# A fused attention and mixture-of-experts kernel: the head of its first pass in another order

## The reference

```python
q = query @ Wq.T + bq;  k = key @ Wk.T + bk;  v = value @ Wv.T + bv
att = where(masks, q @ k.T / sqrt(d), -1e9)
x = x + tanh(g_xattn) * (softmax(att) @ v)      # query = layernorm(x), key = value = ctx
x = x + tanh(g_ffn) * (routed_experts(layernorm(x)) + shared_expert(layernorm(x)))
```

## Time and profile before

| | |
|---|---|
| median of 3 runs | 1158.11 us (1152.9 to 1160.1) |
| profiled execution | 1157.58 us, span 1155.8 us |
| PE busy | 1050.2 us (91%) |
| DVE busy | 822.7 us (71%) |
| ACT busy | 531.4 us (46%) |
| POOL busy | 441.8 us (38%) |
| granted TensorE clock, mean | 0.953 |

### The profile page before, as it was taken

One profiled execution on the slowest core, in us unless ns is written; L12 is line 12 of the kernel. 1 busy time (PEld: TensorE's weight loads), 2 busy tenths in 40 slices (PEclk: granted clock), 3 DMA queues, 4 the chain that ended last, 5 costly groups with the idle time before them and its releaser, 6 DMA issues.

```text
span 1155.8 us, 26617 instructions
## 1 busy us (share of the span) xinstructions
PE 1050.2 (91%) x7344; PEld 677.3 (59%) x7345; DVE 822.7 (71%) x2938; ACT 531.4 (46%) x1041; POOL 441.8 (38%) x654
## 2 busy tenths in 40 slices
PE   4699979999999999860899999999999999999997
PEld 3488767777777777660455555555554444444443
DVE  5899868788888888763576666666665666666666
ACT  1366546666666666640444444444443232232322
POOL 3254647676667667442112112112110423232322
PEclk9999889999999999855899999999999999999999
DMA  7555573223323223432233333333332544444543
GB/s 290 197 177 179 131 173 95 93 93 93 93 93 94 94 93 110 101 102 72 74 110 118 115 113 118 118 109 118 118 109 67 185 158 161 157 168 149 169 149 128
DMA packets 76731, 146.96 MB, mean 127 GB/s; under 512 B 20912, under 2 KB 23088, under 8 KB 73872
## 3 DMA queue, kind: packets, MB, share of 16 engines
q1 hardware_dynamic: 46512, 66.01, 20.0%
q10 hardware_dynamic: 17280, 44.83, 10.5%
q0 software_dynamic: 12896, 35.58, 9.9%
HBM read 94.04 MB, written 52.35 MB: 127 GB/s over the span
## 4 chain that ended last, share of the span: by engine, by line
PE 64%; issue 11%; DVE 9%; POOL 8%; ACT 4%; DMA 2%; POOLq 1%; another core or an unknown queue 1%; SPq 0%; DVEq 0%; ACTq 0%
PE bank L1046 15%; PE bank L1047 15%; PE bank L1048 15%; PE bank L1038 8%; PE bank L1090 3%; PE bank L1108 3%; DVE arena L776 3%; POOL arena L467 3%; POOL token_of_row L503 2%; ACT arena L605 1%; DVE arena L865 1%; POOL arena L474 1%; DMA token_of_row<-arena 1%; DVE peak L879 1%; PE bank L1064 1%
## 5 line engine op out<-in xcount | busy, mean ns | idle before, releaser
L1046 PE MATMUL bank<-weights,arena 128*128 (+1 forms) x682 | 259.9, 381 | 2.1 <-ACT arena L647 1.9
L1047 PE MATMUL bank<-weights,arena 128*128 (+1 forms) x682 | 259.8, 381 | 0.0
L1048 PE MATMUL bank<-weights,arena 128*128 (+1 forms) x682 | 259.6, 381 | 0.0
L1038 PE MATMUL bank<-ident,arena 128*128 128x128 f32 (+1 forms) x1592 | 189.4, 267 | 56.1 <-DMA arena<-normed_rows,arena 25.7
L1038 PEld LDWEIGHTS bank<-ident,arena 128*128 128x128 f32 (+1 forms) x1592 | 161.4, 132 | 103.0 <-issue 71.9
L514 POOL DMA_INDIRECT arena<-normed_rows,arena x71 | 67.1, 946 | 254.9 <-PE bank L1038 238.7
L1108 PEld LDWEIGHTS bank<-arena 128*128 128x128 f32 x1024 | 131.7, 198 | 34.3 <-issue 29.5
L1090 PE MATMUL bank<-arena 128*128 128x512 f32 x256 | 138.8, 647 | 5.4 <-DVE arena L776 5.1
L1108 PE MATMUL bank<-arena 128*128 128x33 f32 x1024 | 128.8, 276 | 2.9 <-issue 1.8
L467 POOL TENSOR_TENSOR arena<-arena 128x512 f32<-128x512 f32 x96 | 101.3, 1056 | 76.8 <-DVE arena L776 75.7
L524 POOL DMA_INDIRECT arena<-expert_rows,arena x64 | 62.8, 981 | 173.9 <-DVE arena L998 156.1
(11 more groups left out here) (175 smaller groups left out, 1895.7 us busy)
## 6 DMA issues: line engine op xcount, KB each, us to landing
expert_rows<-arena ACTq DMA_DIRECT2D x71, 256.0 KB, 2.1
arena<-in_x SPq DMA_DIRECT2D x64, 256.0 KB, 3.2
weights<-in_w_gu ACTq DMA_DIRECT2D x8, 1024.0 KB, 4.7
x_rows<-arena SPq DMA_DIRECT2D x32, 256.0 KB
normed_rows<-arena SPq DMA_DIRECT2D x32, 256.0 KB, 4.9
normed_transposed<-arena SPq DMA_DIRECT2D x32, 256.0 KB, 2.3
arena<-normed_transposed SPq DMA_DIRECT2D x32, 256.0 KB, 3.3
arena<-x_rows SPq DMA_DIRECT2D x32, 256.0 KB, 3.4
```

The source lines that it names most:

```text
L1038: last = t.transpose(dst[:, c * P:(c + 1) * P], src[:, c * P:(c + 1) * P], (ident16 if src.dtype == F16 else ident)[:, :])
L1046: t.matmul(dst, hi[:, rows], w_hi(c), start=(c == 0), stop=False)
L1047: t.matmul(dst, hi[:, rows], w_lo(c), start=False, stop=False)
L1048: last = t.matmul(dst, lo[:, rows], w_hi(c), start=False, stop=(c == chunks - 1))
```

## The change: what it does

SP loads the query weights first, then the small inputs, then context and key weights; the value weights are issued in SP's `beside(1)`, behind the first two tiles. PE computes the keys into banks 2 to 5, then goes straight into the pipeline, and computes the values into banks 6 and 7 in `beside(2)`, after the queries of tile 0. The waits for the low query weights, the router weights, the keys and the values stand at the first product that reads each. DVE makes the low parts of the router and query weights in `beside(0)`, after the statistics of tile 0, and evicts keys and values in `beside(2)`. The reading of the expert chunks starts at iteration 3 in place of 2, so it ends at iteration 11 in place of 10, and ACT's loads of them move by one iteration as well.

```diff
+        K_BANK = 2
-        PEAK_AT, peak_counts = 2, [2, 2, 2, 2, 2, 1, 1, 1, 1]
+        PEAK_AT, peak_counts = 3, [2, 2, 2, 2, 2, 1, 1, 1, 1]
 # SyncE
-            sp.dma_start(ctx_s, ctx_t).then_inc(kv_in, 16)
-            sp.dma_start(wk_s, wk_t).then_inc(kv_in, 16)
+            sp.dma_start(wq_raw, wq_t.rearrange("p c n -> p (c n)")).then_inc(wq_in, 16)
             for dst, src in ((gate_raw[:, :], gates), (bq_s[:, :], bq), (bk_s[:, :], bk), (bv_s, bv),
                              (router_s[:, :, :], router), (pad_raw[:, :, :], pad)):
                 sp.dma_start(dst, src).then_inc(small_in, 16)
-            sp.dma_start(wq_raw, wq_t.rearrange("p c n -> p (c n)")).then_inc(wq_in, 16)
-            sp.dma_start(wv_s, wv_t).then_inc(v_in, 16)
+            sp.dma_start(ctx_s, ctx_t).then_inc(kv_in, 16)
+            sp.dma_start(wk_s, wk_t).then_inc(kv_in, 16)
             def beside(it):
+                if it == 1:
+                    sp.dma_start(wv_s, wv_t).then_inc(v_in, 16)
 # VectorE
-            dve.wait_ge(router_hi, 1)
-            d.scalar_tensor_tensor(router_w[:, 1], ...).then_inc(router_lo, 1)
-            dve.wait_ge(prep_hi, 1)
-            d.scalar_tensor_tensor(wq[:, 1, :], ...).then_inc(prep_lo, 1)
+            def query_weights():
+                dve.wait_ge(router_hi, 1)
+                d.scalar_tensor_tensor(router_w[:, 1], ...).then_inc(router_lo, 1)
+                dve.wait_ge(prep_hi, 1)
+                d.scalar_tensor_tensor(wq[:, 1, :], ...).then_inc(prep_lo, 1)
             def keys_and_values():
-                        d.tensor_scalar(kbd[...], bank[c][...], ...)
+                        last = d.tensor_scalar(kbd[...], bank[K_BANK + c][...], ...)
+                last.then_inc(kv_set, 1)
                 dve.wait_ge(kv_mm, 2)
-                    last = d.tensor_tensor(vaug[:, b, :, 0:D], bank[4 + b][:, :]..., ALU.add)
+                    last = d.tensor_tensor(vaug[:, b, :, 0:D], bank[6 + b][:, :]..., ALU.add)
                 last.then_inc(kv_set, 1)
-                if it == 1:
+                if it == 0:
+                    query_weights()
+                if it == 2:
                     keys_and_values()
 # TensorE
-                    last = t.matmul(bank[co][:, 0:B * T], wk_s[...], ctx_s[:, ci, :], ...)
+                    last = t.matmul(bank[K_BANK + co][:, 0:B * T], wk_s[...], ctx_s[:, ci, :], ...)
             last.then_inc(kv_mm, 1)
-            pe.wait_ge(v_in, 16)
-            for b in range(B):
-                for ci in range(EC):
-                    last = t.matmul(bank[4 + b][:, :], ctx_s[...], wv_s[:, ci, :], ...)
-            last.then_inc(kv_mm, 1)
-            pe.wait_ge(const_set, 11)
-            pe.wait_ge(kv_set, 2)
-            pe.wait_ge(prep_lo, 1)
-            pe.wait_ge(router_lo, 1)
+            def values():
+                pe.wait_ge(v_in, 16)
+                for b in range(B):
+                    for ci in range(EC):
+                        last = t.matmul(bank[6 + b][:, :], ctx_s[...], wv_s[:, ci, :], ...)
+                last.then_inc(kv_mm, 1)
                 # scores(k)
+                        if it_is_first(n, k):
+                            pe.wait_ge(kv_set, 2)
                 # mix_values(k)
+                        if it_is_first(n, k):
+                            pe.wait_ge(kv_set, 3)
                 # queries(chunks)
+                        if it_is_first(n, chunks[0]):
+                            pe.wait_ge(prep_lo, 1)
                 # router
+                    if it_is_first(n6, 0):
+                        pe.wait_ge(router_lo, 1)
+            def it_is_first(n, k):
+                return isinstance(n, int) and n == 0 and k == 0
             def beside(it):
+                if it == 2:
+                    values()
```

More of the change, by code:

```diff
@@ L745, in _ @@
             scale_of(4, 6, 19)
-            dve.wait_ge(router_hi, 1)
-            d.scalar_tensor_tensor(router_w[:, 1], router_s[:, :, :], w_scale[:, 4:5], router_w[:, 0], ALU.mult, ALU.subtract).then_inc(router_lo, 1)
-            dve.wait_ge(prep_hi, 1)
-            d.scalar_tensor_tensor(wq[:, 1, :], wq_raw, w_scale[:, 0:1], wq[:, 0, :], ALU.mult, ALU.subtract).then_inc(prep_lo, 1)
+            def query_weights():
+                dve.wait_ge(router_hi, 1)
+                d.scalar_tensor_tensor(router_w[:, 1], router_s[:, :, :], w_scale[:, 4:5], router_w[:, 0], ALU.mult, ALU.subtract).then_inc(router_lo, 1)
+                dve.wait_ge(prep_hi, 1)
+                d.scalar_tensor_tensor(wq[:, 1, :], wq_raw, w_scale[:, 0:1], wq[:, 0, :], ALU.mult, ALU.subtract).then_inc(prep_lo, 1)
             def keys_and_values():
@@ L756, in keys_and_values @@
                         rows = slice(h * D, (h + 1) * D)
-                        d.tensor_scalar(kbd[rows, :, c, h * T:(h + 1) * T], bank[c][rows, 0:B * T].rearrange("p (b t) -> p b t", b=B),
-                                        bk_s[rows, c:c + 1], float(D) ** -0.5, ALU.add, ALU.mult)
+                        last = d.tensor_scalar(kbd[rows, :, c, h * T:(h + 1) * T], bank[K_BANK + c][rows, 0:B * T].rearrange("p (b t) -> p b t", b=B),
+                                               bk_s[rows, c:c + 1], float(D) ** -0.5, ALU.add, ALU.mult)
+                last.then_inc(kv_set, 1)
                 dve.wait_ge(kv_mm, 2)
                 for b in range(B):
-                    last = d.tensor_tensor(vaug[:, b, :, 0:D], bank[4 + b][:, :].rearrange("p (h d) -> p h d", h=H),
+                    last = d.tensor_tensor(vaug[:, b, :, 0:D], bank[6 + b][:, :].rearrange("p (h d) -> p h d", h=H),
                                            bv_s.rearrange("p (h d) -> p h d", h=H), ALU.add)
@@ L1063, in _ @@
                 for ci in range(EC):
-                    last = t.matmul(bank[co][:, 0:B * T], wk_s[:, ci, co * P:(co + 1) * P], ctx_s[:, ci, :],
+                    last = t.matmul(bank[K_BANK + co][:, 0:B * T], wk_s[:, ci, co * P:(co + 1) * P], ctx_s[:, ci, :],
                                     start=(ci == 0), stop=(ci == EC - 1))
             last.then_inc(kv_mm, 1)
-            pe.wait_ge(v_in, 16)
-            for b in range(B):
-                for ci in range(EC):
-                    last = t.matmul(bank[4 + b][:, :], ctx_s[:, ci, b * T:(b + 1) * T], wv_s[:, ci, :],
-                                    start=(ci == 0), stop=(ci == EC - 1))
-            last.then_inc(kv_mm, 1)
-            pe.wait_ge(const_set, 11)
-            pe.wait_ge(kv_set, 2)
-            pe.wait_ge(prep_lo, 1)
-            pe.wait_ge(router_lo, 1)
+            def values():
+                pe.wait_ge(v_in, 16)
+                for b in range(B):
+                    for ci in range(EC):
+                        last = t.matmul(bank[6 + b][:, :], ctx_s[:, ci, b * T:(b + 1) * T], wv_s[:, ci, :],
+                                        start=(ci == 0), stop=(ci == EC - 1))
+                last.then_inc(kv_mm, 1)
             def body(J, v):
```

## The result

The changed kernel takes 1151.88 us (median of 15 runs, 1148.6 to 1155.2) against 1158.29 of the kernel before in the same comparison (15 runs): ratio 0.9948, 95% interval 0.9927 to 0.9968, so between 3.7 and 8.5 us faster; the medians lie 6.4 apart. That is inside the 1% that was called no change, and close to the 7.3 that the forecast took off. The profiled execution took 1153.63 us with a span of 1151.9, 3.9 shorter than that of before.

A forecast was written before the change was run, and what follows sets the result against it. PE, busy 91% of the span, was taken as the bound, with gains in the head's chain of waits: -10.3 for the head, +1.4 for iteration 7 and +1.6 for the turn gave 1151 us, range 1144.5 to 1158.

The forecast's parts named there:

- part 1: Head, loads: with query weights first and the keys' operands last, keys start at 11.6 instead of 16.00, 4.4 us gained.
- part 2: Head, PE's moved waits: tile 0's rows and the low query weights arrive in time, with slack 3.7 and 5.5, costing nothing.
- part 3: Head: full-speed queries, then values, with evictions under PE's work; DVE starts tile 1 at 33.7, 10.3 us gained including the loads' 4.4.
- part 4: Chunks one iteration later: iteration 7 costs 1.4 us (bounds 0 and 2.27), the turn in iteration 11 costs 1.6 (0 to 3.1).
- The sum: Whole kernel: -10.3 + 1.4 + 1.6 = -7.3 us, giving 1150.3 on the profiled execution and 1150.8 on the median.
- the 1.6 put down for the turn: Turn of the scales, iteration 11: PE and ACT wait 1.6 us more behind the moved chunk, the middle of 0 to 3.1.
- the signs that the forecast named: Wrong if the lead at iteration 3 is under 8, the turn costs over 3, or the lead shrinks in the loop.
- (a): First tile: the clock stays low, costing 1.8 us in the queries and as much in the values, 1154.6; chance 0.15.
- (b): DVE or ACT streams: pauses at new places; one more gives 1155, two 1159.8, slower than before; chance 0.07.
- (c): More gain: one of two pauses disappears and iteration 11's chunk is hidden, 1145.7, or 1144.3 with iteration 7 free; chance 0.2.
- (d): Head: the overlap does not come, only the loads' gain is left, -1.4 us in all, 1156.7; chance 0.08.
- The rule that calls fetches mostly hidden: DVE's and ACT's pauses: by the skill neither is an instruction fetch, and iteration 11's extra chunk costs a plain 1.6 us.

The follow-up runs named there:

- e6: Changed kernel with ScalarE's first pair of chunk loads issued in iteration 2 instead of 1; ratio 0.9988 to the kernel before.
- e7: Changed kernel with the old order of SyncE's loads, so the new order of work alone; ratio 0.9979 to the kernel before.
- after_again: Changed kernel unaltered, run again on another chip; ratio 0.9985 to the kernel before, profiled execution 1156.30 us.
- e10: Changed kernel without the indirect writes of token numbers and the waits for them, so its data are wrong; ratio 0.9634 to the kernel before.
- e2: Kernel before with only the chunk reads and loads moved one iteration later; ratio 1.0041, 4.8 us slower.
- e4: Changed kernel with ScalarE's 3 MB of chunk reloads issued behind the turn of the scales, not in iteration 10; ratio 0.9918 to the kernel before.
- before_again: Kernel before, unaltered, a single run on the chip of the changed kernel's second measurement; profiled execution 1162.63 us.
- e9: Changed kernel with key evictions and chunk reads reordered into VectorE's gaps and the 3 MB reloads behind the turn; ratio 0.9879 to the kernel before.
- e5: Kernel before with only ScalarE's 3 MB of chunk reloads issued behind the turn of the scales; ratio 0.9943, 6.7 us faster on its chip.

## Why the prediction was right, step by step

**Loads (part 1)**: right. Keys start at 11.96 where 11.6 was forecast. The argument that the same bytes are ahead of the key weights as had been ahead of the query weights held to 0.4.

**Waits of PE (part 2)**: right. Tile 0's transposes start as the keys end; no moved wait showed.

**Queries, values and evictions (part 3)**: the mechanism was right, its size 1.7 too large. The step that failed is "from about 23.4, the 16 key evictions", started there as if tile 2's statistics had their rows. I wrote of ACT's moved loads "Nothing", and looked only at whether they come in time for DVE. What they do to the transfer beside them was the missing term: 7.3 us for 256 KB, against 2.5 for tile 4's rows, asked for at 39.46 with no large load just ahead. The profile of before had the row for it: there tile 2's rows, asked for at 24.86 behind ACT's loads of 24.02 and 24.39, landed after 7.1 us, hidden beside the evictions. e6 shows the term by taking it away (1.8 against e4), e7 by having it with other loads.

**Chunks later (part 4)**: right for iteration 8, too low by 0.8. It costs 2.2 (1.4 forecast, 2.27 the upper bound): 8.6 to 6.4 in the changed kernel and the same in after_again, e7 and e10. DVE had no slack there, and a whole chunk is paid. In e2 and e4 it cost 6.1, 3.9 of it by a fall of the clock, which the forecast did not have. At the turn the wait of PE came as forecast (1.94 in e2, 1.53 in after_again, 1.6 forecast), but whether the turn costs anything is open: the pause behind it is shorter with the chunk ahead, as the lower bound of 0 supposed. e2's 4.8 (1.7 to 7.7) fits 2.2 alone, 2.2 + 1.9, and 6.1.

**The sum** by these sizes is -8.6 + 2.2 = -6.4 with nothing for the turn and -4.5 with 1.9 for it, where the profiled execution has -3.9 and the runs -6.4 (-3.7 to -8.5); forecast -7.3. That the time came within 1 us is in part luck: head and iteration 8 together were 2.5 too hopeful, and the 1.6 put down for the turn, which no run shows, made up for most of that. On the chip of after_again the gain was 1.8 by the ratio. In the changed kernel's own execution the wait for tile 11's rows (4.73) and the missing pause nearly cancel, which would have made a look at the turn alone misleading. Of the signs that the forecast named, the lead of 8.6 is above its 8, and what was lost from tile 7 to tile 10 (2.4) is below its 3.

**The rivals.** (a), a low clock in tile 0, did not come: 21 products in a microsecond. (b), more pauses, did not: both kernels have ACT's. Their lengths differ from execution to execution, on one chip too (4.4 in before_again, 5.8 in after_again, 3.7 in e9), so that the change leaves their length alone is not shown. (c) came in one half: DVE's pause is gone in the profile of the changed kernel and in e7, but it is there in after_again (2.47), and iteration 8 was not free. (The lower end of the range stands as 1144.5, where its sum gives 1144.3.) (d) did not: the evictions lie under the values, but for the wait.

**The rule that calls fetches mostly hidden.** At the turn my suspicion was of a fetch. The pause there is missing without the 3 MB of reloads (e4, e5, e9) and without the scatter (e10), ACT's only without the scatter. The profile counts the packets of queue q8, which it calls instruction. In 115 to 125 us, just ahead of and at the start of ACT's pause, it has in the changed kernel, and then in e10:

```profile
q8 instruction: 1, 0.02, 4.2%
...
q8 instruction: 1, 0.02, 0.6%
```

The last number is the share of 16 engines' time in 10 us: the one packet took 6.7 us, and 1.0 without the scatter. So packets of instructions are held up in that stretch. That the engine waits for them is not shown: in e4 the packet took 1.6 (1.0% of 120 to 130 us) and ACT paused for 6.08. The cause of the pauses stays open; the Trainium skill, "Runtime: NRT & Kernel Launch", section "Instruction fetch mechanics", is neither confirmed nor refuted.

## What to carry to other kernels

When the order of a set-up is changed, cost each moved transfer twice: when it must be there, and which small transfer it runs beside; here 2 MB asked for 0.8 us ahead of a tile's rows cost 1.7 us through an eviction queued behind that tile. Look in the profile of before for a transfer that already runs beside such a load. Work that has been moved "one later" arrives at a place with another slack: two chunk reads cost nothing in a gap of the head, and a single one its full length where the engine is 97% busy. Look for an engine's idle stretch first and put the work there: the same pieces in VectorE's gaps, with the large reloads away from the serial turn, gave 0.9879 where the change gave 0.9948 and 0.9985.

## What the runs showed that was not expected

- Three loads of 1 MB issued one iteration ahead of a serial exchange between engines cost 6.7 us in the kernel before (ratio 0.9943, interval 0.9919 to 0.9967). In the changed kernel tile 11's rows were asked for at 137.24 beside them, and VectorE, which stood waiting, had them at 155.16, 17.9 us later.
- The same kernel, the same gap of 2.5 us in PE, and the granted clock fell to 0.50 behind it in one execution and stayed at 1.00 in another; price 1.7 us. In iteration 8 the same happened behind gaps that the moved chunk makes: two of seven executions with the moved chunk paid 3.9 us more (e2, e4).
- Writing the token numbers, 128 times 4 bytes and twice for each tile, with the waits for it, costs the first pass 1.0 us in each iteration behind tile 11 (14.3 against 13.3 on the same chip) and more around the pauses. By tile 31 that is 27.2, some four times the 6.4 that this change gained.
